# Attention 2: query pairs turned by halves of four tiles, and a rounding that writes the three copies of the queries

## The reference, cut

```python
def _fq_sym(x, axis):
    s = jnp.maximum(jnp.max(jnp.abs(x), axis=axis, keepdims=True) / 127.0, 1e-8)
    return jnp.clip(jnp.round(x / s), -127.0, 127.0) * s
...
q = (x @ Wq + bq).reshape(1, B * N, H, hd)                 # x is layer-normed
kv = (cond @ Wkv + bkv).reshape(1, -1, 2, H, hd)
q = _fq_sym(jnp.transpose(q * scale, (0, 2, 1, 3)), axis=-1)
k = _fq_sym(k, axis=-1);  v = _fq_sym(v, axis=2)
attn = jax.nn.softmax(jnp.einsum('bhqd,bhkd->bhqk', q, k), axis=-1)
out = jnp.einsum('bhqk,bhkd->bhqd', _fq_unsigned(attn, axis=-1), v)
```

## Time and profile before

| what | us |
|---|---|
| median of 3 runs (lowest, highest) | 895.12 (892.81, 899.02) |
| the profiled execution, its own time | 893.93 |
| its span, first to last instruction | 892.2 |
| last normalised tile of `xn` done, before attention 2's queries | 230.2 |
| first scores of attention 2 on PE | 260.69 |
| busy in the span: PE, DVE, ACT, POOL | 747.1, 547.6, 371.8, 364.2 |
| mean granted TensorE clock, as a share of full | 0.929 |

### The profile page before, as it was taken

How to read it: one execution, slowest core, us unless ns; L and a number is a source line. 1 busy time by engine, 2 the same in 40 slices (tenths; PEclk the granted TensorE clock), 3 DMA queues, 4 the chain that set the end, 5 groups by cost and what they waited for, 6 DMA issues and landing times.

```text
span 892.2 us, 15038 instructions
## 1 busy us (share of the span) xinstructions
PE 747.1 (84%) x5517; PEld 496.0 (56%) x5517; DVE 547.6 (61%) x1290; ACT 371.8 (42%) x674; POOL 364.2 (41%) x387
## 2 busy tenths in 40 slices
PE   5998899994778878787889799298697769999997
PEld 3444554562635555455555588145255437787776
DVE  3897847337689999999936655395798750000014
ACT  4002023222479989898923133334275313221210
POOL 2941220463047878776700570554032044000124
PEclk9999999997887979988889999699999969999999
DMA  7501127898009999999941375810004125433513
GB/s 239 195 0 48 31 48 213 227 132 72 1 10 175 179 152 185 158 185 161 175 133 48 76 148 119 293 39 8 1 1 186 51 57 170 137 129 109 168 42 119
DMA packets 139730, 103.09 MB, mean 116 GB/s; under 512 B 109857, under 2 KB 124697, under 8 KB 137611
## 3 DMA queue, kind: packets, MB, share of 16 engines
q1 hardware_dynamic: 130756, 79.36, 36.4%
q0 software_dynamic: 7984, 22.16, 12.7%
q10 hardware_dynamic: 918, 0.62, 0.2%
HBM read 65.60 MB, written 11.33 MB: 86 GB/s over the span
## 4 chain that ended last, share of the span: by engine, by line
PE 28%; DVE 12%; issue 9%; POOL 6%; ACT 4%; DMA 3%; POOLq 0%; DVEq 0%; ACTq 0%
PE psum L2414 7%; PE psum L2434 5%; PE psum L1639 3%; PE psum L1654 2%; PE psum L2439 1%; DVE xnT L1427 1%; ACT both L1320 1%; PE psum L132 1%; PE psum L1234 1%; POOL both L573 1%; POOL both L440 1%; POOL both L1789 1%; PE psum L223 1%; DVE both L2233 1%; PE psum L1497 1%
## 5 line engine op out<-in xcount | busy, mean ns | idle before, releaser
L1427 DVE TENSOR_SCALAR_CACHE_REDUCE xnT<-psum,both 128x1024 bf16<-128x1024 f32 x128 | 158.0, 1281 | 16.8 <-PE psum L1234 16.4
L1320 ACT ACTIVATE both<-psum,both 128x1024 f32<-128x1024 f32 x128 | 153.7, 1208 | 15.2 <-DVE xnT L1427 14.8
L1131 POOL TENSOR_SCALAR both<-both 128x1024 f16<-128x1024 f32 x128 | 133.7, 1045 | 48.3 <-ACT both L1320 38.3
L1234 PE MATMUL psum<-both 128*128 128x512 bf16 x256 | 89.1, 436 | 28.2 <-ACT both L1320 25.5
L2511 DVE COPY both<-psum 128x256 f32<-128x256 f32 (+1 forms) x21 | 8.0, 381 | 123.8 <-PE psum L2434 113.4
L1255 PEld LDWEIGHTS psum<-both 128*128 128x128 f16 x1024 | 64.7, 99 | 27.5 <-issue 13.4
L132 PE MATMUL psum<-identb 128*128 128x512 bf16 x217 | 60.1, 421 | 22.9 <-DVE x L970 12.4
L1255 PE MATMUL psum<-both 128*128 128x16 f16 x1024 | 68.8, 172 | 10.8 <-DVE xn L1436 7.3
L573 POOL DMA_INDIRECT both<-moe_y_dram,moe_idx_from x48 | 46.3, 965 | 73.6 <-DMA moe_y_dram<-both 47.1
L2414 PE MATMUL psum<-both 128*128 128x320 f32 x256 | 72.3, 436 | 0.2 <-ACT both L561 0.2
L2475 ACT ACTIVATE both<-psum 128x320 f32<-128x320 f32 x64 | 28.0, 437 | 103.6 <-PE psum L2414 103.6
(11 more groups left out here) (383 smaller groups left out, 1519.2 us busy)
## 6 DMA issues: line engine op xcount, KB each, us to landing
both<-in_l_experts SPq DMA_DIRECT2D x50, 384.0 KB, 4.2
both<-in_l_experts SPq DMA_DIRECT2D x16, 1024.0 KB, 5.5
grouped_y_dram<-both SPq DMA_DIRECT2D x31, 128.0 KB
ctok<-in_ctx SPq DMA_DIRECT2D x2, 1024.0 KB, 7.3
both<-kpad_dram SPq DMA_DIRECT2D x1, 2048.0 KB, 8.1
moe_xn_dram<-xn POOLq DMA_DIRECT2D x4, 512.0 KB, 3.9
moe_y_dram<-both POOLq DMA_DIRECT2D x7, 256.0 KB, 5.2
both<-both SPq DMA_TRANSPOSE x96, 3.4
```

Of the source, the lines that this page charges most:

```text
L1131: nc.gpsimd.tensor_scalar(r2[n % RSLOTS2], e2[:, n % ESLOTS2, :], 255.0, HALF_BASE, ALU.mult, ALU.add).then_inc(sem("r2_ready"), 1)
L1234: last = nc.tensor.matmul(bank[2 * (n % SRING2) + half], qz2[:, h % 2, h // 2, t * P:(t + 1) * P], kT2[:, h // 2, half * 512:(half + 1) * ...
L1320: nc.scalar.activation(e2[:, n % ESLOTS2, :], scores_at(n), ACT.Exp, bias=bias2[:, n:n + 1], scale=s2[:, t * H2 + h:t * H2 + h + 1], accum ...
L1427: nc.vector.tensor_scalar(scaled2[n % 2], scores_at(n), ns2[:, t * H2 + h:t * H2 + h + 1], None, ALU.mult, ALU.min, accum_out=bias2[:, n:n ...
```

## The change

The preparation is cut into halves throughout, and the work is dealt to the engines in another way:

- PE projects the first half of the tiles (`project(0)`) before it turns the second half of `xn`; key pairs are turned two at a time between these steps. ACT copies the first half of `xnT` ahead of the key pairs 0 to 3, and the second half between key pairs 3 and 4.
- Each half of the queries is turned on its own: `turn_queries(0)` takes tiles 0 to 3 of all eight pairs (four transposes each, banks 4 to 7) once the first half is quantised, `turn_queries(1)` tiles 4 to 7 (banks 0 to 3).
- Of the first half ACT copies both the lower and the upper partitions, 16 copies of 64x512. Of the second half DVE copies the eight upper parts and the lower parts of pairs 0 to 4 (`LOW_BY_VECTOR2`), ACT the lower parts of pairs 5 to 7.
- In the quantisation the step that scaled the reciprocal is folded into the product (`scalar_tensor_tensor`), the negative scales are made once for both halves, and the rounding writes the three bf16 copies itself.
- POOL zeroes the first half of `qz2`'s pads as soon as `qa2`'s are zeroed; only the other half waits for the queries, and only the ninth step of the loop for it. The `awake` counts are 10, 3 x 4 and 6 instead of 8, 6, 14 and 10.

```diff
-            def turn_pairs(src, numbers):
...
+            def turn_queries(half):
+                for n in range(PAIRS2):
+                    if half == 0 and n == 4:
+                        pe.wait_ge(sem("qkf2_ready"), 8)
+                    if half == 0 and n >= 4:
+                        awake(3, 3)
+                    if half == 0:
+                        pe.wait_ge(sem("qkT2_ready"), PAIRS2 + n - 3)
+                    elif n >= 4:
+                        pe.wait_ge(sem("qT2_ready"), 2 * (n - 3))
+                    for t in range(4):
+                        last = nc.tensor.transpose(bf(4 - 4 * half + n % 4)[:, t * P:(t + 1) * P],
+                                                   qa2[:, 4 * half + t, 2 * n:2 * n + 2, :].rearrange("p a b -> p (a b)"), identb[:])
+                    last.then_inc(sem("qkT2_blocks"), 1)
...
-            turn_pairs(ka2, range(4))
-            ln_tensor(pe, 2, lambda: awake(6, 2))
-            project(0, xnT, wq2[:], True)
-            turn_pairs(ka2, range(4, H2 // 2))
+            turn_keys(range(2))
+            ln_tensor(pe, 2, first_queries)
+            turn_keys(range(4, 6))
+            project(1)
+            turn_keys(range(6, PAIRS2))
...
+            turn_queries(0)
+            pe.wait_ge(sem("v2_ready"), 2)
+            pe.wait_ge(sem("qkf2_ready"), 8)
             pe.wait_ge(sem("qa2_ready"), 2)
-            turn_pairs(qa2, range(H2 // 2, H2))
-            awake(10, 2)
...
+            turn_queries(1)
+            pe.wait_ge(sem("qkT2_ready"), 2 * PAIRS2)
+            awake(6, 7)
+            pe.wait_ge(sem("pads2_ready"), 2)
+            pairs_copied(pe)
...
-            ln_scalar(act, 2, lambda: copy_pairs(range(4)))
-            copy_pairs(range(4, H2 // 2))
+            for part in range(2):
+                root_scalar(act, 2, part)
+            for half in range(2):
+                evacuate_T(act, xnT, sem("xnT_blocks"), sem("xnT_ready"), turned(2), half)
+                copy_keys(range(4 * half, 4 * half + 4))
...
-            copy_pairs(range(H2 // 2, H2))
+            copy_queries(range(PAIRS2), 0)
+            copy_queries(range(LOW_BY_VECTOR2, PAIRS2), 1)
...
-                seq.mark(nc.vector.tensor_scalar(ns2[:, some], s2[:, some], -1.0, None, ALU.mult))
-                seq.step(times2(qf, is2[:, some]))
-                seq.step(round2(qf))
-                nc.vector.tensor_copy(qa2[:, four, :, 0:3 * HD2].rearrange("p t h (a d) -> p (t h) a d", a=3),
-                                      bcast(qf.rearrange("p t (h d) -> p (t h) d", h=H2), 2, 3)).then_inc(sem("qa2_ready"), 1)
+                q3 = qf.rearrange("p t (h d) -> p (t h) d", h=H2)
+                seq.step(nc.vector.scalar_tensor_tensor(q3, q3, HD2 ** -0.5, bcast(is2[:, some], 2, HD2), ALU.mult, ALU.mult))
+                nc.vector.tensor_scalar(qa2[:, four, :, 0:3 * HD2].rearrange("p t h (a d) -> p (t h) a d", a=3),
+                                        bcast(q3, 2, 3), MAGIC, MAGIC, ALU.add, ALU.subtract).then_inc(sem("qa2_ready"), 1)
...
+            for n in range(PAIRS2):
+                dve.wait_ge(sem("qkT2_blocks"), 2 * PAIRS2 + n + 1)
+                nc.vector.tensor_copy(qz2[ROWS:P, 1, n, 512:T], bf(n % 4)[ROWS:P, 0:512]).then_inc(sem("qT2_ready"), 1)
+                if n < LOW_BY_VECTOR2:
+                    nc.vector.tensor_copy(qz2[0:ROWS, 0, n, 512:T], bf(n % 4)[0:ROWS, 0:512]).then_inc(sem("qT2_ready"), 1)
```

More of the change, by code:

```diff
@@ L1156, in l1x_turn_sync, with pairs_copied @@
               .then_inc(sem(f"rT2_ready{n % RSLOTS2}"), 16)
[L1158 to L1162, removed]
+        PAIRS2 = H2 // 2
+        LOW_BY_VECTOR2 = 5
+        def pairs_copied(eng):
+            eng.wait_ge(sem("qkT2_ready"), 3 * PAIRS2 - LOW_BY_VECTOR2)
+            eng.wait_ge(sem("qT2_ready"), PAIRS2 + LOW_BY_VECTOR2)
         def l1x_values_tensor(pe):
@@ L1183, in l1x_tensor, with project @@
         def l1x_tensor(pe):
[L1184 to L1188, removed]
+            def project(half):
+                pe.wait_ge(sem("xnT_ready"), 8 + 2 * half + 2)
+                for t in range(4 * half, 4 * half + 4):
                     for c in range(DC):
-                        last = nc.tensor.matmul(bank[first + t // 2][:, t % 2 * D:(t % 2 + 1) * D], src[:, c, t * P:(t + 1) * P],
-                                                w[:, c, :], start=(c == 0), stop=(c == DC - 1))
+                        last = nc.tensor.matmul(bank[t // 2][:, t % 2 * D:(t % 2 + 1) * D], xnT[:, c, t * P:(t + 1) * P],
+                                                wq2[:, c, :], start=(c == 0), stop=(c == DC - 1))
@@ L1192, in project, with turn_keys @@
                     if t % 2:
                         last.then_inc(sem("qk2_done"), 1)
-            def turn_pairs(src, numbers):
-                for n in numbers:
+            def turn_keys(pairs):
+                for n in pairs:
                     if n >= 4:
-                        pair_copied(pe, n - 4)
+                        pe.wait_ge(sem("qkT2_ready"), n - 3)
                     for t in range(NT):
                         last = nc.tensor.transpose(bf(4 + n % 4)[:, t * P:(t + 1) * P],
-                                                   src[:, t, 2 * (n % 8):2 * (n % 8) + 2, :].rearrange("p a b -> p (a b)"), identb[:])
+                                                   ka2[:, t, 2 * n:2 * n + 2, :].rearrange("p a b -> p (a b)"), identb[:])
@@ L1214, in l1x_tensor, with first_queries @@
+            def first_queries():
+                turn_keys(range(2, 4))
+                project(0)
+            moe0.wait(pe, "added", NT * K0 - 5)
+            awake(10, 0)
+            pe.wait_ge(sem("ka2_ready"), 1)
+            turn_keys(range(2))
[3 more added lines that the diff above has]
+            turn_keys(range(6, PAIRS2))
+            pe.wait_ge(sem("qkf2_ready"), 6)
             for t in range(NT):
@@ L1232, in scores @@
                     pe.wait_ge(sem("e2_ready"), n - SRING2 + 1)
+                if n == NT:
+                    pe.wait_ge(sem("pads2_ready"), 3)
                 for half in range(2):
@@ L1297, in l1x_scalar, with copy_keys, copy_queries @@
                 nc.scalar.copy(ka[:, :, i * HD2:(i + 1) * HD2], kd).then_inc(sem("ka2_high"), 1)
-            def copy_pairs(numbers):
-                for n in numbers:
+            def copy_keys(pairs):
+                for n in pairs:
                     act.wait_ge(sem("qkT2_blocks"), n + 1)
-                    if n < H2 // 2:
-                        nc.scalar.copy(kT2[:, n, :], bf(4 + n % 4)).then_inc(sem("qkT2_ready"), 1)
-                    else:
-                        nc.scalar.copy(qz2[0:ROWS, 0, n % 8, :], bf(4 + n % 4)[0:ROWS]).then_inc(sem("qkT2_ready"), 1)
-            ln_scalar(act, 2, lambda: copy_pairs(range(4)))
-            copy_pairs(range(4, H2 // 2))
+                    nc.scalar.copy(kT2[:, n, :], bf(4 + n % 4)).then_inc(sem("qkT2_ready"), 1)
+            def copy_queries(pairs, half):
+                some = slice(512 * half, 512 * half + 512)
+                for n in pairs:
+                    act.wait_ge(sem("qkT2_blocks"), (1 + half) * PAIRS2 + n + 1)
+                    ps = bf(4 - 4 * half + n % 4)
+                    low = nc.scalar.copy(qz2[0:ROWS, 0, n, some], ps[0:ROWS, 0:512])
+                    if half == 0:
+                        nc.scalar.copy(qz2[ROWS:P, 1, n, some], ps[ROWS:P, 0:512]).then_inc(sem("qkT2_ready"), 1)
+                    else:
+                        low.then_inc(sem("qkT2_ready"), 1)
+            for part in range(2):
[3 more added lines that the diff above has]
+                copy_keys(range(4 * half, 4 * half + 4))
             for b in range(2):
```

20 lines of the change are left out of this document (5 added, 15 removed).

## The result

The changed kernel takes 889.32 us (median of 14 runs) against 896.32 for the kernel before beside it, a ratio of 0.9924 (95% interval 0.9908 to 0.994): 5.4 to 8.2 us less. The prediction said 888, with 884.5 to 893 as its range and 6.0 us of gain. That the spans differ by just the 6.0 us of the forecast is partly luck: the stretch begins 1.65 us later, its first maximum comes 5.98 us earlier counted from there, the loop takes 0.3 us more, and the stages behind it take 2.0 us less.

The account below looks back on a forecast made before the run. The bound was the chain projection, two quantisations, eight query-pair copies ahead of attention 2's loop. Earlier projection, shorter quantisation and overlapped copies put first scores at 254.7 instead of 260.69: 893.93 - 6.0 = 887.9, said as 888; range 884.5 to 893.

Parts of the forecast that it names:

- The earlier projection: PE before the quantisation: `project(0)` starts at 229.15 instead of 232.65, second bias add at 232.75 at the high clock.
- first open value: PE's clock at `project(0)`: high was taken; the low clock puts the second bias add at 234.4, worth 1.7 us.
- The shorter quantisation: DVE's quantising of queries: each half takes 1.07 us less, ending at 238.65 and 245.1; three-output rounding 1.76 us.
- The copies: Query copies to the first scores: ACT's 16 at 0.61 each end at 252.9, its last three 254.5, DVE's 13 254.4.
- second open value: Whether ACT's alternating lower and upper copies overlap: no overlap taken, 252.9 and 254.5; with overlap 250.8 and 252.4.
- rival 1: Query copies overlap on both engines: scores at 253.0, 7.7 us less, 886.2; chance 0.18.
- The last awake: PE's `awake(6, 7)` ahead of the scores: 252.9 to 254.3, 1.4 us, hidden by copies; at low clock ends 255.7.
- rival 2: PE's clock low at `project(0)` and again in the thin stretch of four transposes: gain 3.2, 890.7; chance 0.14.
- third move: Before the first scores: the first half's query copies run beside the second quantisation; no separate size given.
- DVE or PE waiting for ACT in the second half: Listed among the signs that would show the forecast wrong, in the second half of the queries; no size given.
- Rival 3: The loop of attention 2 gives the gain back: four more low-clock stretches lose 6.4 us, five give 895.9; chance 0.07.
- Rival 4: A half query copy costs a whole one: 19 copies at 0.91 end at 260.4, no gain, 893.8; chance 0.03.

Follow-up runs that it names:

- e5: The changed kernel with the projection and ACT's copies of `xnT` put back where they were, query halves and short quantisation kept; ratio to the kernel before 0.9982.
- e9: The kernel before with the earlier projection alone (quantisation, whole query pairs and zeroing as before); ratio to the kernel before 0.9945.
- e10: The changed kernel run once more, unaltered; 890.36 us, ratio to the kernel before 0.9931.
- e2: The changed kernel with query pairs turned and copied whole after the second half is quantised, early projection and short quantisation kept; ratio to the kernel before 0.9917.
- e3: The kernel before with only the shorter quantisation (scale folded into the product, rounding writes three copies, negative scales once); ratio to the kernel before 0.9978.

## Why the prediction was right, and where it was not

1. *The earlier projection* was right to 0.1 us, clock included: the second bias add comes 3.94 us from the row of `xn`, which is where 232.75 in the frame of before put it. The first open value fell on the high clock, in this profile and in the nine profiles of experiments that have the early projection (first half 3.72 us in each). The reason given for that choice, an idle time of 1.3 us where the clock had fallen after 1.5, is not shown: the changed kernel's clock stays at 1.00 through 1.84 us of idle ahead of 245.36, and e5's through 1.96. The earlier projection is the largest part, 5.15 us by itself (e9).
2. *The shorter quantisation* was right in its size: the second half of the chain takes 6.50 us, 6.5 was said. The rounding with three outputs runs at the pace of the copy, 1.76. The first half took 6.63 instead of 5.9, for POOL's zeroing, which the prediction put under "what costs nothing": it did not look for what POOL disturbs on DVE. That made the second half 0.7 us late, which ACT's copies covered.
3. *The copies*: without overlap, 0.60 and 0.455 apart (0.61 and 0.43 were said), so the second open value fell as taken, from two rows at the kernel's end, and rival 1 fell with it. ACT began at 13.65, 0.6 us earlier than worked out, and ended at 24.77 instead of 25.7.
4. *The last awake* was said to be hidden, and was not: the clock fell at 253 in the thin stretch of four transposes at a time, the awake ended 1.2 us after the copies. That is the second half of rival 2. It cancels the 0.9 us of point 3: the first maximum came at 26.66, where 25.9 + 0.76 was said. That agreement is luck, two errors that cancel. In e10, where the clock fell later, the first maximum came at 26.44.
5. *The reason* given for the third move was wrong. "What bounds the kernel" said that the change lets the copies of the first half run beside the second quantisation. They do, but it gains nothing (e2 against the changed kernel, and e5 against e3, whose first maximum is 0.5 us earlier without the halves). The sum hid this because it went straight from the chain before to the chain after and never worked out the chain with whole pairs: 16.99 + 0.75 + 7.38 is 25.1, nearly the same as the copies by halves (24.77). Nor was ACT nearly without work beside the two quantisations before, as that paragraph has it: it copied keys and values for 5.7 of those 14.5 us. And the sign "DVE or PE waiting for ACT in the second half" came true (2.01 us on DVE) without the sum being wrong, because the sum itself has that wait, from 245.1 to 248.8.
6. *Rival 3*, that the loop gives the gain back, fell: 182.2 to 183.5 us in the twelve other profiles, 182.9 before. Rival 4 fell with the copies of 0.58.
7. *The 9 us* that the prediction put as what a measurement can tell from no change were too many: with 14 runs of each kernel the interval is 1.4 us to either side, and the 6.8 us of the ratio are clear of it.

Left open: what moves the stages behind the loop by up to 5 us from one execution to the next was not looked into, and neither was the start of the stretch, 228.1 to 234.1. Whole pairs with the early projection, the short quantisation and the late zeroing, which might be a simpler kernel of the same speed, were not run.

## What to carry to other kernels

Where a change does several things, work out the chain with each of them alone before you name the cause: here one of three, the order of two copies on ACT ahead of the projection, held nearly all of the gain. Cutting work into halves to overlap it only helps if the engine that does the extra, smaller instructions is not the one that binds. And when an effect is smaller than the scatter of the whole, measure it as a distance between two rows of the stretch that it acts on.

## What the runs showed of the hardware

- An ACT copy of 64x512 from PSUM takes 0.58 us. The next one begins after 0.48 if it works on the same partitions, and after 0.60 if it goes from the lower to the upper 64 or back. On DVE the same copies, 0.43, stand 0.34 apart ((1.11 - 0.43) / 2) or 0.455. The Trainium skill, "VectorE: DVE Perf Modes", section "Two Vector instructions with no wait between them", has the rule that the prediction told, and DVE's numbers agree with it. ACT's copies show the same pattern.
- A DVE instruction on 64 numbers waited 0.7 us for the end of a POOL zeroing (0.90 us, and 0.20 without the zeroing beside it), while a reduction of 1.22 us just before it was not held up.
- In the changed kernel PE's clock stayed at 2.4 GHz through 1.14 us of idle ahead of the projection and through 1.84 us ahead of 245.36. In the kernel before it fell within 1.96 us of idle; in e5 it outlived an idle time of the same length and fell 1.2 us later, while PE was busy. So the length of one idle time does not tell these cases apart. In the thin stretch it fell at different places in different executions of the same program: at 253.0, with the last transposes, in the changed kernel, and in its second execution (e10) only within the last `awake`.
